# A two-layer transformer kernel on one core: the first chunk's q placed on chip, its score maxima added by one-hot matmuls, feed-forward weights loaded from the start, and the planner's tables set anew

## The reference, cut to what matters

```
# layer 0
xn = layernorm(x)
q, k, v = split(xn @ Wqkv)              # 32 heads of 16 for q; one head of 16 for k and for v
scores = q k^T / 4 + alibi, causal      # per head, 256 x 256
x = x + softmax(scores) v @ Wo          # softmax needs each row's maximum
      + top-2 of 4 LoRA experts of xn   # rank 16, gates by softmax
# layer 1
xn = layernorm(x)
q = xn Wq + bq (16 x 32 per token); k, v = 16 per token
o[d] = sum_e softmax_e(q[d, h] k[e] / 4) v[e]; broadcast o over the heads
h = silu(xn G^T) * (xn U^T)             # G, U: 1792 x 512 int32 weights times row scales
x = x + o + h D^T                       # D: 512 x 1792
```

## Time and profile before

| what | us |
|---|---|
| device time, median of 3 runs | 624.78 (624.44 to 625.1) |
| span of the profiled execution, first to last instruction | 623.2 |
| PE busy in that span | 570.7 (92%) |
| DVE busy | 461.3 (74%) |
| ACT busy | 377.0 (61%) |
| POOL busy | 351.7 (56%) |

### The profile page before, as it was taken

The page is one execution under the profiler, slowest core; times in us unless marked ns, Lnnn a source line. Parts: engine busy times, 40 slices in busy tenths (PEclk is TensorE's granted clock), DMA queues, the critical chain, the costliest instruction groups (busy, mean ns, idle before and its releaser), DMA issues.

```text
span 623.2 us, 14286 instructions
## 1 busy us (share of the span) xinstructions
PE 570.7 (92%) x5590; PEld 421.3 (68%) x5590; DVE 461.3 (74%) x1034; ACT 377.0 (61%) x703; POOL 351.7 (56%) x364
## 2 busy tenths in 40 slices
PE   4579583699999999999999999999999999999997
PEld 4466451467885668776968587858685876785783
DVE  4769874899999874899697748996986569354642
ACT  3287095847875478675757485858684776651240
POOL 6231595724655667674837574848576677542140
PEclk9987895599999999999999999999999999999999
DMA  8767799905054146001610160016001000000000
GB/s 207 152 95 78 123 237 217 170 2 54 2 54 87 37 68 70 3 4 35 88 17 5 35 86 4 4 35 88 1 5 52 18 1 9 28 2 2 35 1 34
DMA packets 98942, 34.97 MB, mean 56 GB/s; under 512 B 75548, under 2 KB 90044, under 8 KB 98876
## 3 DMA queue, kind: packets, MB, share of 16 engines
q1 hardware_dynamic: 76044, 24.58, 22.7%
q0 software_dynamic: 2352, 7.18, 5.7%
q10 hardware_dynamic: 20480, 2.31, 2.6%
HBM read 30.19 MB, written 8.39 MB: 62 GB/s over the span
## 4 chain that ended last, share of the span: by engine, by line
PE 68%; DVE 13%; SPq 8%; ACT 4%; issue 3%; DMA 2%; POOL 2%; ACTq 1%; DVEq 0%
PE B_bank L1266 27%; PE B_bank L1287 14%; PE A_bank L1218 7%; SPq L693 5%; PE A_bank L1191 4%; DVE mx L1537 4%; PE A_bank L1120 3%; PE E_bank L1176 3%; PE B_bank L1154 3%; PE E_bank L1171 2%; PE B_bank L1254 1%; DMA qq<-nmp 1%; ACTq L693 1%; SPq L731 1%; SPq L717 1%
## 5 line engine op out<-in xcount | busy, mean ns | idle before, releaser
L883 POOL TENSOR_TENSOR probs<-e,probs 128x512 f16<-128x512 f32 x176 | 208.3, 1188 | 127.2 <-ACT probs L999 126.8
L1266 PE MATMUL B_bank<-xs,wgu 128*128 128x256 f16 x1792 | 204.3, 273 | 0.3 <-DVE hf L1649 0.3
L998 ACT ACTIVATE e<-E_bank,wn 128x512 f32<-128x512 f32 x192 | 133.7, 696 | 103.4 <-PE E_bank L1176 53.9
L1266 PEld LDWEIGHTS B_bank<-xs,wgu 128*128 128x128 f16 x1792 | 172.7, 98 | 21.6 <-DVE hf L1649 0.6
L999 ACT ACTIVATE probs<-E_bank,wn 128x512 f16<-128x512 f32 x192 | 134.0, 698 | 0.0
L1287 PE MATMUL B_bank<-wd,hbuf 128*128 128x512 f16 x448 | 99.9, 379 | 0.1
L897 POOL TENSOR_TENSOR hbuf<-hf,hbuf 128x512 f16<-128x512 f32 x56 | 65.8, 1176 | 56.2 <-ACT hbuf L1033 55.8
L1537 DVE TENSOR_REDUCE mx<-B_bank 128x2 f32<-128x384 f32 (+5 forms) x168 | 92.1, 603 | 4.5 <-PE B_bank L1154 4.4
L1639 DVE SCALAR_TENSOR_TENSOR hf<-ebuf,B_bank 128x512 f32<-128x512 f32 x56 | 38.3, 684 | 62.2 <-ACT ebuf L1043 61.9
L1287 PEld LDWEIGHTS B_bank<-wd,hbuf 128*128 128x128 f16 x448 | 43.2, 98 | 49.3 <-POOL hbuf L897 0.6
L1043 ACT ACTIVATE ebuf<-B_bank,sgx 128x256 f32<-128x256 f32 x112 | 47.5, 485 | 22.1 <-PE B_bank L1266 20.8
(11 more groups left out here) (199 smaller groups left out, 696.3 us busy)
## 6 DMA issues: line engine op xcount, KB each, us to landing
qq<-q_parts SPq DMA_DIRECT2D x21, 256.0 KB
x<-in_x SPq DMA_DIRECT2D x20, 256.0 KB, 3.1
out_y<-x SPq DMA_DIRECT2D x16, 256.0 KB, 2.0
xa<-in_x SPq DMA_DIRECT2D x12, 256.0 KB, 5.1
q_parts<-qs SPq DMA_DIRECT2D x48, 64.0 KB, 2.9
wgu<-in_gate_w POOLq DMA_DIRECT2D x4, 448.0 KB, 9.1
wgu<-in_up_w POOLq DMA_DIRECT2D x4, 448.0 KB, 8.7
wd<-in_down_w POOLq DMA_DIRECT2D x4, 448.0 KB, 7.1
```

The source lines that it names most:

```text
L883: pool.tensor_tensor(probs[:, u % PSLOTS, 1, :], e32[:, w, :], probs[:, u % PSLOTS, 0, :], ALU.subtract).then_inc(s_lop, 1)
L998: act.activation(e32[:, w, :], psum("exp", i, g, w)[:, :], ACT.Exp, scale=wn[:, 7:8])
L1266: mm = pe.matmul(psum(name, u, i)[:, a * SEQ:(a + 1) * SEQ].rearrange("p (t n) -> p t n", t=NU), wgu[:, m, k, (2 * i + a) * P:(2 * i + a + ...
```

## The change

1. **q of chunk 0 stays on chip.** `store` and `gather_first` are gone. A step `place(b, m)` on SP copies a q tile by three DMAs from SBUF to SBUF into `natural[m]` (space lent by wd, hf, attnT and x1), and a step `place(b, m)` on DVE copies it into qq (48 partitions x 2048, f16). For the four tiles of b = 1 SP waits until the same `natural[m]` has been emptied.
2. **Maxima of sequence 0.** Groups of two heads' worth in the order of q tiles (`FIRST_MAXG`, 32 groups instead of 21), so that a group waits for its own tile alone. They are transposed in two halves (`nm0`), split by ACT and DVE into `nm_first`, and stay in SBUF: after every score matmul of sequence 0, one-hot matmuls of 128 columns (`pick`) add the maxima in PSUM, four for each exp, 96 in all. The transposed maxima of the other sequences go by DMA as before.
3. **Weights.** The eight gate and up loads wait for nothing and stand in POOL's order from the first layernorm on; the turned wq that lay in their place lies in xs. The four down loads and `late` 2 to 8 wait for `place(1, 3)`. The first gate matmul waits for gate and up alone, the first `half` for down.
4. **Small things.** The position and slope tables move from DVE (L1389, L1390) to ACT; the load of a second identity goes; mask and key constants are loaded ahead of x tiles 2 and 3; a memset moves from POOL to DVE; `hi`/`lo` take wtok first; the statistics of x tile t of a chunk wait for `xn0` of the tile before; x1 loads 4 and 5 wait for `place(1, 3)`.
5. **Tables.** Every entry of `US` and `RANK` is set anew.

```diff
-POOL_OF = {... "norm2": "E", "q0": "A", ...
+POOL_OF = {... "norm2": "E", "nm0": "A", "q0": "A", ...
+FIRST_MAXG = [(tb, 2 * n, 2) for n in range(NK) for tb in range(NTB)]
+HI_ORDER = [NK, 0, 1, 2, 3] + list(range(NK + 1, 2 * NK + 2))
...
-      "DVE": {"norm": 0.2, "scale": 1.3, "tables": 2.2, "scaled": 0.4, "hot": 0.64, "ln0": 0.84, "xn0": 0.6, "tok": 1.1, "q": 0.7,
+      "DVE": {"norm": 0.2, "scale": 1.3, "tables": 0.9, "place": 0.7, "nm0": 0.3, "scaled": 0.4, "hot": 0.64,
+             "ln0": 0.8, "xn0": 0.6, "tok": 0.82, "q": 0.62, "mix": 2.9, "mixb": 3.4, "norm2": 0.2, "scale2": 2.44,
...
-            def store(b, m):
-                wait_used(act, "q0", b, m)
-                store_heads(act, 0, b, m, q_first[:, b, m, :, :], s_q0[b][m])
...
-            def gather_first(m):
-                gather_heads(sp, 0, (m,), PART_Q, 0)
+            def place(b, m):                                     # SP
+                if b:
+                    sp.wait_ge(s_placed, m + 1)
+                for g, part in enumerate(PART_Q):
+                    if part == 0:
+                        sp.wait_ge(s_q0h, b * NK + m + 1)
+                    else:
+                        wait_used(sp, "q0", b, m)
+                    sp.dma_start(natural[m][g * HD:(g + 1) * HD, :].rearrange("d (h t) -> d h t", t=SEQ),
+                                 q_first[:, b, m, part, :]).then_inc(s_natural[m], 16)
...
+            def place(b, m):                                     # DVE
+                dve.wait_ge(s_natural[m], 48 * (b + 1))
+                dve.tensor_copy(qq[0:R_ALIBI, b, :, 8 * m:8 * m + 8, :],
+                                natural[m][0:R_ALIBI, :].rearrange("d (h c t) -> d c h t", c=NTB, t=GT)).then_inc(s_placed, 1)
...
             def exp(i, g, w):                                    # PE
-                if g == 0 and w == 0:
-                    pe.wait_ge(s_nmrow[b], 32 * (c + 1))
+                if i == 0 and g % (NHG // 2) == 0 and w == 0:
+                    wait_used(pe, "nm0", 0, g // (NHG // 2))
+                if i and g == 0 and w == 0:
+                    pe.wait_ge(s_nmrow[b], 32 * (c + b))
...
+                    for c1 in range(0 if i else blocks):
+                        row = g // 2 % 2 * 2 * NTB + 2 * (t0 + c1) + g % 2
+                        mm = pe.matmul(acc[:, c0 + c1, :, :], pick[:, row:row + 1].broadcast_to([NG, P]),
+                                       nm_first[:, g // (NHG // 2), :].rearrange("r (h t) -> r h t", t=GT), start=False, stop=True,
+                                       skip_group_check=True)
...
             def late(n):
                 if n == 2:
-                    pool.wait_ge(s_nmrow[0], 32)
-                    pool.wait_ge(s_wlo, NK + 1)
+                    pool.wait_ge(s_placed, 2 * NK)
+                    pool.wait_ge(s_wlo, 1)
...
             def ffn_load(n):
                 k = n // 2
-                if n == 0:
-                    pool.wait_ge(s_gather[1], 16 * 3)
+                if n == 2 * NK:
+                    pool.wait_ge(s_placed, 2 * NK)
...
-                        pe.wait_ge(s_ffn, 16 * N_FFN)
+                        pe.wait_ge(s_ffn, 16 * 2 * NK)
```

314 lines of the change are left out of this document (173 added, 141 removed), and 19 rows, old and new, of tables (RANK, US).

## The result

The changed kernel is slower: 652.9 us, median of 4 runs (649.23 to 654.92), against 624.94 for the kernel before in 4 runs of the same comparison. The ratio is 1.0429, with a 95% interval of 1.0389 to 1.047. The prediction was 612.0, with a range of 601 to 623 and a chance of 0.12 for slower: it was wrong in sign, and the upper end of the range was passed by 30 us.

What follows compares the result with a forecast made beforehand. PE work behind the first gate matmul was taken as nearly fixed, so only bringing the gate forward or moving PE work ahead pays: 623.2 - 11.8 - 1.1 = 610.3 span, 612 us with 1.6 for the median; range 601 to 623.

Steps and rivals of the forecast that it cites:

- An us is won or lost ahead of the gate: Whole kernel: PE work behind the first gate matmul is nearly fixed, 1.1 us less there; gate 11.8 us sooner.
- DVE's work: Ahead of the gate: DVE's work rises from 114.7 to about 122.5 us, place copies at 0.72 us each.
- The scale: Start: the scale of the weights comes at 24.5, 3.2 us late, 3 us added for eight early loads.
- rival C: Start: loads hold x and wq 7 us more, or place copies cost nearer 2.27; 619 to 626 us; chance 0.14.
- First q: Second stage: place copies land in some 2.8 us; with 5 us DVE idle the last placed tile is in place at 52.
- POOL's hold: After the last placed tile: POOL's gaps, 5.92 and 7.00 us, delay the first low part to about 73; ACT stands 64 to 74.
- Rival B: Ahead of the gate: no POOL hold, exps flow once maxima are there; 603 us (599 to 606); chance 0.12.
- the other 21 go at the pitch of ACT's pair: Sequence 0: its remaining exps take 1.14 us each, 24.0 us; last exp at 103.2, 12.0 us sooner.
- were late anyway: SP, first q: later q stores wait for the last placed tile, but had been late before; no cost given.
- Last exp to gate: Stretch from sequence 0's last exp to the gate: same steps, left at 36.4 us; gate at 139.6.
- the picks: Sequence 0's exps on PE: 96 one-hot matmuls at most 0.104 us each, 10.0 us, fit barely in 14.1 us free.
- Rival D: PE clock between scale and gate: below 0.625 the kernel is slower, 630 us at 0.60, 657 at 0.5; chance 0.12.

Runs made afterwards that it cites:

- late_weights: Changed kernel with the eight gate and up loads moved behind the last split of wq in POOL's order: 642.97 us, ratio 1.0265 to the kernel before.
- later_down: Changed kernel, all-reduce early, sequence 1's maxima ahead of the gather, gate/up loads behind exp (0, 2, 0), down loads behind exp (1, 1, 1): 629.12 us, ratio 1.007.
- early_reduce: Changed kernel with the all-reduce's setup steps moved earlier on DVE and POOL: 649.06 us, ratio 1.0368 to the kernel before.
- both_moves: Changed kernel with the moves of late_weights and early_reduce together: 646.31 us, ratio 1.0301 to the kernel before.
- gather_first: Changed kernel, all-reduce early, gate/up loads split behind exps (0, 2, 0) and (1, 0, 1), down behind (1, 1, 1), maxima behind gather: 625.19 us, ratio 0.9976.
- max_later: later_down with sequence 2's first eight maxima groups behind the third chunk's third-tile transposes on PE and DVE: 629.77 us, ratio 1.0068.
- max_later2: As max_later, but on PE sequence 2's first ten maxima groups stand behind sequence 1's seventh exp: 627.11 us, ratio 1.0017.

## Why the prediction was wrong, step by step

**Right.** *An us is won or lost ahead of the gate*: the rest took 471.18 us, 0.7 less than before, where 1.1 less was said. *DVE's work* ahead of the gate: 122.45 us, 122.5 said; a place copy took 0.69, as the hot copy (0.72). That it meets to a tenth is partly luck: the hot copies took 6.7 us, 1.2 more than before. *The loads' issues were not held.* By the rule of SBUF — State Buffer, "SBUF: two separate sides", in the Trainium skill, DVE's two-port copies keep POOL from writing the descriptors of its DMAs. The prediction left that out of its sum, and for the issues the trace bears this out: they took 0.54 to 0.86 us each (0.61). The trace agrees with the page for a small step of POOL beside the first three hot copies, 1.27 us where the same step took 0.42 before. Copies stretched too, five to 4.77 us. The power for the scale began at 24.96, when the last of them had ended, so its 0.56 us says nothing on this.

```profile
15.18 1.27 POOL L884 TENSOR_SCALAR rs<-mv 128x1 f32<-128x1 f32 x1 [1.83 <-DVE mv L1448]
```

```profile
18.93 4.77 DVE L1442 COPY qq<-hot 64x2048 f16<-64x2048 f16 x5
```

**Where the 41.8 us went.** The gate came at 181.4 instead of 139.6. By the table of events, 5.9 of the difference were there at the scale, 14.4 more came up to the last placed tile, 7.0 up to the first low part, 6.1 in sequence 0's exps (35.1 us from 101.5 to 136.6, where 29.2 was said) and 8.4 behind them.

**Wrong, "The scale".** The eight loads' extra was put at 3 us on a landing of at most 6.7; the x tile of the chain took 15.12. The scale came at 30.4. In late_weights, without these loads, it came at 26.1, so 1.6 of the 5.9 us was not theirs. 30.4 lay inside the bounds that the prediction kept and was its sign of rival C; but C priced the start at 7 us and ended at 626.

**Wrong, "First q".** This is the step that failed by most. It priced the place copies, 2.8 us each, and not the queue ahead of them, which it put at nothing. Six DMAs stand there on SP. Beside the loads they took it 26.5 us to issue where before they took 9.0, and 9.7 in late_weights. The earlier trace rows had shown it: four small stores take SP 23.66 us beside the same loads. I read that as a cost of the stores; it is one of the loads, and goes where they go. "2.8" was wrong too for the first copy, which took 8.58 us to land; the copies of that first tile took up to 6.8 in late_weights too, so not all of this is the loads'. "5 us idle" became 14.84 in one wait on DVE and 18.9 in all its waits up to the last tile, which was in place at 72.3, not 52. Taking the loads away from the start returns 10 us (late_weights), the scale included, and less what they cost in their later place.

**Mis-sized, "POOL's hold".** The mechanism was right and both gaps came back, as a wait of ACT after three exps; but from 73.2 instead of 52, and 7.75 and 11.13 us long instead of 5.92 and 7.00. Of the 27.3 us by which the first low part came after the forecast, 21.2 are the late start and 5.9 the longer gaps. Rival B is refuted by that. So is the reading on which it rested: GPSIMD Engine Reference, 2.1 "Instruction dispatch", in the Trainium skill, gives the 6 us for the first call to freshly loaded code, but here the return from custom code to ordinary work was paid again, 11.13 us in the changed kernel, and 7.06 in later_down, where the all-reduce stood early:

```profile
44.64 0.73 POOL L850 TENSOR_TENSOR wm<-wm,mhalf 128x2 f32<-128x2 f32 x1 [7.06 <-issue]
```

**Left out, what is late next.** Had the hold been taken away, "the other 21 go at the pitch of ACT's pair" would still have failed: a q tile of the second chunk stands in ACT's list among them, and waits for a store (9.19 and 20.89 us in early_reduce and both_moves). I wrote that the later q stores "were late anyway", and didn't ask who waits for them.

**Wrong, "Last exp to gate", "I leave it 36.4".** It took 45.5 (135.90 to 181.42; before 114.49 to 151.35, 36.9). The maxima of sequence 1 had been made by 104.3, ahead of sequence 0's last exp; the new order makes them behind it, so their transpose, split and two DMAs now lie on the path. Of the 8.7 us more, 7.4 lie between sequence 0's last and sequence 1's first exp (12.9 against 5.5). In gather_first the stretch takes 152.8 - 106.9 = 45.9, again with 12.9 there.

**Wrong, the picks.** "At most 0.104 each": they took 13.4 us, 0.14 each. The group by form, 60 to 140 us:

```profile
L1214 PE MATMUL E_bank<-nm_first,pick 64*128 64x128 f16 x96 | 13.4, 239 | 0.0
```

In gather_first, with the long waits gone, they fill PE: it is busy 37.74 of 38.56 us, and sequence 0's exps take 37.9 (69.1 to 106.9) against 35.5 before. No run takes the picks away, so their share in that is not measured. Of the 9.9 us by which its first exp comes sooner, its last keeps 7.6, and the gate none: 9.0 are lost behind that exp.

**Rival D** is not the cause of the main loss. The clock was 0.70, 0.78 and 0.81 in the three stages; weighted by PE's work (32.60, 40.33 and 37.59 us) the mean is 0.77, above the 0.70 that the forecast needed, and over the whole way from scale to gate 0.76, not under 0.65. Before, the mean by work was 0.81; at that, PE's work here would take some 5 us less (an estimate: 110.5 x (1 - 0.77 / 0.81) = 5.5). How much of it lay on the path is not shown.

Summed up: gather_first has all the edits, with five changes of order on POOL and DVE, and returns all 28 us. The edits themselves gain nothing that can be measured. In gather_first's trace the first exp is 9.9 us sooner than before; 2.4 of that go in sequence 0's exps, where PE is full, and 9.0 behind them, 7.3 of these between the two sequences, where the maxima of sequence 1 are no longer hidden. And the loads met some queue of small transfers at nearly every place tried.

## What to carry to other kernels

Before a large load is moved, list what each issuing queue holds at its new place: transfers in short runs beside it, and whatever stands behind them on that queue, were held up here, mostly by 5 to 20 us, nearly wherever the load went. When a wait is taken away, follow each engine's own list to the next instruction that waits for a transfer; its wait is the new price. Before an order is changed by hand to fill a wait, look for the wait's origin: by their ratios, from later_down on, filling the hole gave nothing in max_later and 3 us in max_later2, and letting its transfer go sooner (with the loads divided at the same time) 6.
